# First batch's gate product in three rounded passes, with its low halves made on GpSimd

## The chip, the cores and the metric

One core of a Trainium2 chip runs the kernel. The metric is the device time of one execution in microseconds (us). The engines are TensorE (PE; its weight loads are listed apart as PEld), VectorE (DVE), ScalarE (ACT), GpSimd (POOL) and SyncE (SP, which here only issues DMAs). Each works through its own instructions in order; they are tied together by semaphores.

## The reference, cut to what matters

```python
x = L0_attn_x                                   # (16 batches, 512 tokens, 256 channels)
h = layernorm(x) * (1 + ca) + sa                # modulation of the batch
u, gate = split(h @ W_in.T)                     # the gate product is this second half
b_t = u @ W_state.T
decay = exp(-min(softplus(u @ W_dt.T + b_dt), 10) * rate)
hs = scan(decay, b_t)                           # h = d*h + (1-d)*b, over the 512 tokens
y = hs @ W_C.T
z = y * silu(gate) + h * D
x = x + ga * (z @ W_out.T)
h = layernorm(x) * (1 + cb) + sb
xr, xk = mu_r*h + (1-mu_r)*h_prev, mu_k*h + (1-mu_k)*h_prev
x = x + gb * sigmoid(xr @ W_r.T) * (square(relu(xk @ W_k.T)) @ W_v.T)
```

Everything is float32.

## The kernel before

A batch is a tile of 256 channels x 512 tokens, held as two halves (CH = 2) of 128 partitions x 512 columns. `half(outs, w, at, x, c)` (line 293 does its matmuls) multiplies input half c by the weights of each of the output halves, so a full 256 x 256 product is two calls with two matmuls each.

A product is made in one of two ways. Unsplit, both operands are float32; the profile shows each such matmul of 512 columns as two instructions. In three rounded passes, the input x is split into a rounded part x_hi (type fp32r, a copy) and x_lo = x - x_hi, the weights w likewise, and w_hi x_hi + w_lo x_hi + w_hi x_lo is summed in PSUM; each of these matmuls is one instruction. Batch 0 uses the unsplit form for its front products (dt, b), its gate product and its state output; from batch 1 on the front and gate products have three passes, and most others do from batch 2 on. The second block of the reference ("receptance" xr and "key" xk) has three passes for all batches but the last one's key.

The order on each engine is written out by hand: a prologue for batches 0 to 2, and then a loop over steps s, which works at once on batches a = s, b = s-1, c = s-2 and d = s-3. s = 3 is the first step, with d = 0, c = 1, b = 2 (WHOLE = 2).

What the change and the steps of the prediction touch:

- TensorE: in the prologue the front products of batch 0 (`w_front`), its gate product with `modulation(4, 3)` between its halves, `state_out(0)` (line 333; it waits for the scan of batch 0), `first_norm(1)` (transposes, line 300), `modulation(7, 5)`, `attention_out(0, 0)` (it waits for z of batch 0), `front_high(1)`, `front_low(1)` (which waits for both h_lo of batch 1), `attention_out(0, 1)`, `first_norm(2)`, `gate_high(1)`, `gate_low(1)`, `token_stats(0)`, `state_out(1)`, and `gate_high(2)`, which waits for `silu_ok` 2. In the loop the products of the receptance xr with the low halves xr_lo, and the state's products (lines 527, 528, 537).
- ScalarE: `modulated(0, i)` writes h of batch 0 (line 667), then `exponential(0)` (688), `decays(0)` (692, 697), a table load, `ln1_apply(1)` (658), `gate_silu(0)` (719), the rounded weights wl_hi (740), h and h_hi of batch 1 (684).
- VectorE: the rounded and low parts of the weights wf (1060 to 1065), three operations on a 128x1 rate (1067, 1069, 1071), the statistics of batch 1 (894), `clipped(0)` (983), means and variances (901), `driven(0)` (988), `scanned(0)` (996), `ln1_apply(1)` (909), statistics of batch 2, `gated(0)` (1001, and z in 1009), `ln1_apply(2)` (909), both h_lo of batch 1 (1084), the rest of the modulation, `clipped(1)`.
- GpSimd: `ln1_scale(k)` (1181 to 1188) makes the scale and shift of batch k out of VectorE's variances and is waited for by `ln1_apply(k)`; `weight_low_part(n, at)` (1203) makes wl_lo out of wl_hi; `low_part` (1173) makes xk_lo, xr_lo, k_lo; `low_state` (1227) state_lo; `second_scale(c)` (1211 to 1222) the scale of the second norm.
- The rate's sum on VectorE is `nc.vector.tensor_tensor(rate[:, 0:1], rate[:, 0:1], rate[:, 2:3], ALU.add)` (line 1069): two inputs in SBUF, one element a partition.

Of the kernel before, what the change touches and what calls it, by code (L numbers as in the profile page):

```python
# [7 lines left out]
F32 = mybir.dt.float32  # L8
F32R = mybir.dt.float32r
BF16 = mybir.dt.bfloat16  # L10
ALU = mybir.AluOpType
# [9 lines left out]
def before(eng, sem, count):  # L21

    if count > 0:
        eng.wait_ge(sem, count)

def adaln_block(nc, x_tok_d, x_ch_d, w_d, wmod_d, c_d, cols_d, ident_d, out_d):
    NB, C, T = x_ch_d.shape
    CH = C // P
    TT = T // P  # L30
    NS = P
    EXP_MAX = float(np.expm1(DT_MAX))

    with ExitStack() as ctx:
# [3 lines left out]
        def sem(name):  # L38
            return ctx.enter_context(nc.semaphore(name))
# [9 lines left out]
        wf_hi = sb("wf_hi", [P, CH, 2 * NS + C], F32R)  # L49
        wf_lo = sb("wf_lo", [P, CH, 2 * NS + C], F32R)  # L50
        wl_hi = sb("wl_hi", [P, CH, 4 * C], F32R)
        wl_lo = sb("wl_lo", [P, CH, 4 * C], F32R)
        h_hi = sb("h_hi", [P, CH, T], F32R)
        h_lo = sb("h_lo", [P, CH, T], F32R)
# [4 lines left out]
        xr_hi = sb("xr_hi", [P, CH, T], F32R)  # L59
# [140 lines left out]
        row_spread_ok, row_rstd_ok, rows_ok, offset_ok, root_ok = sem("row_spread_ok"), sem("row_rstd_ok"), sem("rows_ok"), sem("offset_ok"), sem("root_ok")  # L200
        scaled1_ok = sem("scaled1_ok")
        minus1_ok = sem("minus1_ok")
        spread1_ok, slo_ok, rstd1_ok, shift1_ok, rstd2_ok, first_ok = sem("spread1_ok"), sem("slo_ok"), sem("rstd1_ok"), sem("shift1_ok"), sem("rstd2_ok"), sem("first_ok")
        hlo_ok, zlo_ok, xklo_ok, xrlo_ok, klo_ok = sems("hlo_ok"), sems("zlo_ok"), sems("xklo_ok"), sems("xrlo_ok"), sems("klo_ok")

# [6 lines left out]
        def live(k):  # L212
            return 0 <= k < NB
# [7 lines left out]
        def split_state(k):  # L221
            return WHOLE <= k <= LAST
# [66 lines left out]
        def _(pe):  # L289
            def half(outs, w, at, x, c, first=False, last=False):  # L290

                for d, out in enumerate(outs):
                    ins = nc.tensor.matmul(out, w[:, c, at + d * P:at + (d + 1) * P], x[:, c, :], start=first, stop=last)  # L293
                return ins
# [118 lines left out]
            half(dt_out, w_front, 0, h[:, 0], 1, last=True).then_inc(dt_ps, 1)  # L413
            half(b_out, w_front, NS, h[:, 0], 0, first=True)
            half(b_out, w_front, NS, h[:, 0], 1, last=True).then_inc(b_ps, 1)
            pe.wait_ge(s_wgate, 16)
            g_out = [ps_gate(0)[:, d, :] for d in range(CH)]
            half(g_out, w_early, GATE, h[:, 0], 0, first=True)
            pe.wait_ge(s_wmod2, 16)
            modulation(4, 3, slot[2][:, 1, :])  # L420
            half(g_out, w_early, GATE, h[:, 0], 1, last=True).then_inc(g_ps, 1)
            pe.wait_ge(s_wy, 16)
            state_out(0)
            first_norm(1)
# [27 lines left out]
            for s in STEPS:  # L452
# [68 lines left out]
                if live(b):  # L521
# [6 lines left out]
                            nc.tensor.matmul(ps_y[:, i, :], wy_lo[:, i * P:(i + 1) * P], state_hi[:], start=False, stop=False)  # L528
                    else:
                        state_out(b)  # L530
                if live(d) and d > 0:
                    pe.wait_ge(xrlo_ok[1], d + 1)
                    half(r_out, wl_hi, MIX_R, xr_lo, 1, last=True).then_inc(r_ps, 1)
                if split_state(b):
# [13 lines left out]
                if live(c) and c < LAST:  # L548
                    pe.wait_ge(xn2b_ok, c + 1)
                    to_channels(ps_n, xn2, range(TT // 2, TT)).then_inc(t3_ps, 1)  # L550
                if d == 0:
                    pe.wait_ge(xrlo_ok[1], d + 1)
                    half(r_out, wl_hi, MIX_R, xr_lo, 1, last=True).then_inc(r_ps, 1)
                if d == LAST:
                    for done in xr_ok:
                        pe.wait_ge(done, d + 1)
# [79 lines left out]
        def _(act):  # L636
# [29 lines left out]
            def modulated(k, i):  # L666
                return nc.scalar.activation(h[:, k % 2, i, :], ps_h(k)[:, i, :], ACT.Identity, bias=mod_at(SHIFT1 + i, k), scale=mod_at(SCALE1 + i, k))
# [11 lines left out]
            def rounded_h(k):  # L679
                act.wait_ge(h_ok, k + 1)  # L680
                before(act, ghi_ps, k - 1)
                if k == WHOLE + 1:
                    act.wait_ge(b_ps, k)
                nc.scalar.copy(h_hi[:], h[:, k % 2]).then_inc(hhi_ok, 1)  # L684

            def exponential(k):
                act.wait_ge(dt_ps, k + 1)
                nc.scalar.activation(ps_front[:, 0, :], ps_front[:, 0, :], ACT.Exp, bias=col(B_DT)).then_inc(e_ok, 1)
# [41 lines left out]
            modulated(0, 0).then_inc(h0_ok, 1)  # L730
            act.wait_ge(t1_ps, 1)
            modulated(0, 1).then_inc(h_ok, 1)
            exponential(0)
            decays(0)
            nc.scalar.preload_act_table_set("silu_and_others")
# [433 lines left out]
        def _(pool):  # L1169
            def low_part(lo, x, hi, there, used, done, k):  # L1170
                pool.wait_ge(there, k + 1)
                before(pool, used, k)
                nc.gpsimd.tensor_tensor(lo, x, hi.bitcast(F32), ALU.subtract).then_inc(done, 1)  # L1173

            def ln1_scale(k):

                pool.wait_ge(mv1_ok, k + 1)
                before(pool, xn1a_ok, k - 1)
                before(pool, xn1b_ok, k - 1)
                if k > 0:  # L1180
                    nc.gpsimd.tensor_scalar(spread1[:, k % 2, 0, :], mv1[:, k % 2, :, 0], -1.0, None, ALU.mult)
                nc.gpsimd.tensor_scalar(spread1[:, k % 2, 1, :], mv1[:, k % 2, :, 1], EPS, None, ALU.add).then_inc(spread1_ok, 1)
                pool.wait_ge(spread1_ok, k + 1)
                nc.gpsimd.tensor_tensor(rstd1[:, k % 2], spread1[:, k % 2, 1, :], half_neg[:], ALU.pow).then_inc(rstd1_ok, 1)
                pool.wait_ge(rstd1_ok, k + 1)
                if k == 0:
                    pool.wait_ge(minus1_ok, 1)
                nc.gpsimd.tensor_tensor(shift1[:, k % 2], spread1[:, k % 2, 0, :], rstd1[:, k % 2], ALU.mult).then_inc(shift1_ok, 1)
# [12 lines left out]
            def weight_low_part(n, at):  # L1201
                pool.wait_ge(wl_hi_ok, n)
                nc.gpsimd.tensor_tensor(wl_lo[:, :, at:at + C], w_late[:, :, at:at + C], wl_hi[:, :, at:at + C].bitcast(F32), ALU.subtract).then_inc(wl_lo_ok, 1)
# [20 lines left out]
            def low_state(k):  # L1224
                pool.wait_ge(shi_ok, k - WHOLE + 1)
                pool.wait_ge(y_ps, k)
                nc.gpsimd.tensor_tensor(state_lo[:], state[:], state_hi[:].bitcast(F32), ALU.subtract).then_inc(slo_ok, 1)
# [11 lines left out]
                last.then_inc(offset_ok, 1)  # L1239

            ln1_scale(0)
            ln1_scale(1)
            pool.wait_ge(mod1_ok, 1)
            nc.gpsimd.tensor_scalar(scale_neg[:], mod[:, SCALE1:SCALE1 + CH, :], -float(np.sqrt(C)), None, ALU.mult)
            nc.gpsimd.tensor_scalar(scale_root[:], mod[:, SCALE1:SCALE1 + CH, :], float(np.sqrt(C)), None, ALU.mult).then_inc(root_ok, 1)
            weight_low_part(1, MIX_K)
            ln1_scale(2)
            weight_low_part(2, MIX_R)
            ln1_rows(WHOLE + 1)
            low_h(2, 0)  # L1250
# [9 lines left out]
            for s in STEPS:  # L1260
                a, b, c, d = s, s - 1, s - 2, s - 3
                if live(d) and d < LAST:
                    low_part(xk_lo[:, 0], xk[:, 0], xk_hi[:, 0], xkhi_ok[0], k_ps, xklo_ok[0], d)
                    low_part(xk_lo[:, 1], xk[:, 1], xk_hi[:, 1], xkhi_ok[1], k_ps, xklo_ok[1], d)
                if c == 1:
                    second_scale(c)
                if live(d):
                    low_part(xr_lo[:, 0], xr[:, 0], xr_hi[:, 0], xrhi_ok[0], r_ps, xrlo_ok[0], d)
                if b == WHOLE:
                    low_state(b)  # L1270
                if live(a + 1) and a > WHOLE + 1:
                    ln1_rows(a + 1)
                if c == LAST:
                    low_part(xr_lo[:, 1], xr[:, 1], xr_hi[:, 1], xrhi_ok[1], r_ps, xrlo_ok[1], d)
                if live(c) and c > 1:
                    second_scale(c)
                if live(d) and c != LAST:
                    low_part(xr_lo[:, 1], xr[:, 1], xr_hi[:, 1], xrhi_ok[1], r_ps, xrlo_ok[1], d)
                if split_state(b) and b > WHOLE:
                    low_state(b)  # L1280
                if live(d) and d < LAST:
                    for i in range(CH):
                        low_part(k_lo[:, i], k_act[:, i], k_hi[:, i], kact_ok, v_ps, klo_ok[i], d)
                if d == LAST:
                    pool.wait_ge(rv_ok, d + 1)
                    pool.wait_ge(s_out[d % 2], 16 * (d // 2))
                    nc.gpsimd.tensor_tensor(x2[:, d % 2, 0], rv, x1[:, d % 3, 0, :], ALU.add).then_inc(x2_ok[0], 1)
                if live(a) and a > WHOLE:
                    low_h(a, 0)
                if split(b):  # L1290
                    for i in range(CH):
                        pool.wait_ge(zhi_ok[i], b - WHOLE + 1)
                        pool.wait_ge(o_ps, b)
                        nc.gpsimd.tensor_tensor(z_lo[:, i], z[:, i], z_hi[:, i].bitcast(F32), ALU.subtract).then_inc(zlo_ok[i], 1)  # L1294
                if live(a) and a > WHOLE:
                    low_h(a, 1)
# [37 lines left out]
```

## Time and profile before

| | us |
|---|---|
| median of 3 runs | 343.72 |
| lowest, highest | 343.62, 874.88 |
| the profiled execution | 343.59 |
| its span | 341.8 |

```profile
PE 335.0 (98%) x1574; PEld 265.4 (78%) x1574; DVE 303.6 (89%) x465; ACT 292.4 (86%) x393; POOL 275.5 (81%) x274
PE   8999998999999999999999999999999999999995
PEclk9999999999999999999999999999999999999999
```

The first line is each engine's busy time, its share of the span and its instructions. The others cut the span into 40 equal slices (8.5 us each): a digit is the busy share in tenths, and PEclk is the granted clock of TensorE in tenths of full speed. A timeline row is: start, duration, engine, line, operation, output<-inputs, shapes, count, and in brackets how long the engine had idled before it and what ended that. Rows with a count are merged, and their duration is from the first start to the last end. Rows of one engine can overlap a little, since an instruction starts while the one before drains. Times are counted from the start of the span.

### The profile page before, as it was taken

The numbers are of one execution on the slowest core, as the hardware profiler recorded it, in microseconds if no ns is written. First come the engines' busy times: TensorE is split into PE (matmuls) and PEld (weight loads), VectorE is DVE, ScalarE is ACT, GpSimd is POOL, SyncE is SP. The second block draws the span as 40 slices with busy tenths as digits, with TensorE's granted clock in tenths as the row PEclk, the third lists the DMA queues.
The fourth block names the chain that finished last, engine by engine and source line by source line (L and its number), as shares of the span: only waits on it lengthen the run. The fifth ranks groups of instructions, "written<-read, shape, count | busy, mean of one in ns | idle before, by whom it ended". The sixth has DMA issues, their size and how long they took to land.

```text
span 341.8 us, 5185 instructions
## 1 busy us (share of the span) xinstructions
PE 335.0 (98%) x1574; PEld 265.4 (78%) x1574; DVE 303.6 (89%) x465; ACT 292.4 (86%) x393; POOL 275.5 (81%) x274
## 2 busy tenths in 40 slices
PE   8999998999999999999999999999999999999995
PEld 4567676788888888888888888888888888887764
DVE  3789888999999999999999999999999989887846
ACT  4486778989999999999999998999999999888484
POOL 2151879989898998989899898989899896966752
PEclk9999999999999999999999999999999999999999
DMA  7960523060513406051421505151320501010013
GB/s 276 416 226 13 172 83 104 1 221 27 186 61 112 136 18 221 11 186 63 161 85 64 186 0 186 63 186 61 102 83 14 174 3 61 1 63 0 2 60 126
DMA packets 18556, 36.00 MB, mean 105 GB/s; under 512 B 4960, under 2 KB 5728, under 8 KB 18400
## 3 DMA queue, kind: packets, MB, share of 16 engines
q1 hardware_dynamic: 17808, 35.19, 29.7%
q10 hardware_dynamic: 720, 0.48, 0.5%
q8 instruction: 13, 0.21, 0.3%
q14 instruction: 15, 0.12, 0.1%
HBM read 27.22 MB, written 8.44 MB: 104 GB/s over the span
## 4 chain that ended last, share of the span: by engine, by line
PE 89%; DVE 5%; issue 3%; ACT 2%; POOL 0%; DVEq 0%; ACTq 0%; POOLq 0%
PE slot L293 71%; PE slot L386 4%; PE slot L300 4%; PE slot L537 2%; PE slot L528 2%; PE slot L527 2%; PE slot L307 1%; PE slot L314 1%; PE slot L333 1%; DVE xk L979 1%; DVE xr L979 1%; DVE xn L945 1%; PE slot L394 1%; DVE h L940 0%; ACT prev L663 0%
## 5 line engine op out<-in xcount | busy, mean ns | idle before, releaser
L1173 POOL TENSOR_TENSOR k_lo<-k_act,k_hi 128x512 fp32r<-128x512 f32 x30 | 50.2, 1694 | 4.5 <-ACT k_act L872 4.5
L663 ACT ACTIVATE prev<-slot,mod,mix_prev 128x512 f32<-128x512 f32 x64 | 46.4, 785 | 1.3 <-PE slot L300 0.7
L293 PE MATMUL slot<-h_hi,wf_hi 128*128 128x512 f32 x120 | 43.0, 399 | 0.1
L1173 POOL TENSOR_TENSOR xr_lo<-xr,xr_hi 128x512 fp32r<-128x512 f32 x32 | 42.7, 1337 | 0.2 <-ACT xr_hi L709 0.2
L293 PE MATMUL slot<-h_hi,wf_lo 128*128 128x512 f32 x120 | 41.9, 390 | 0.0
L1173 POOL TENSOR_TENSOR xk_lo<-xk,xk_hi 128x512 fp32r<-128x512 f32 x30 | 38.6, 1315 | 3.7 <-ACT xk_hi L703 3.7
L1232 POOL TENSOR_TENSOR h_lo<-h,h_hi 128x512 fp32r<-128x512 f32 x28 | 36.5, 1305 | 1.3 <-ACT h_hi L684 1.3
L1294 POOL TENSOR_TENSOR z_lo<-z,z_hi 128x512 fp32r<-128x512 f32 x26 | 33.3, 1303 | 2.7 <-ACT z_hi L858 2.7
L293 PE MATMUL slot<-h_lo,wf_hi 128*128 128x512 f32 x120 | 34.2, 389 | 0.0
L979 DVE SCALAR_TENSOR_TENSOR xk<-slot,mix_new,prev 128x512 f32<-128x512 f32 x32 | 23.8, 746 | 8.2 <-issue 7.9
L945 DVE TENSOR_SCALAR xn<-slot,stats,rstd 128x256 f32<-128x256 f32 x62 | 29.2, 532 | 0.0
L725 ACT ACTIVATE k_act<-slot 128x1024 f32<-128x1024 f32 x15 | 15.5, 1031 | 14.1 <-PE slot L293 14.1
L293 PEld LDWEIGHTS slot<-h_hi,wf_hi 128*128 128x128 f32 x120 | 22.4, 188 | 6.1 <-issue 1.4
L293 PEld LDWEIGHTS slot<-h_hi,wf_lo 128*128 128x128 f32 x120 | 22.5, 188 | 5.3 <-issue 0.5
L1001 DVE TENSOR_TENSOR slot<-silu,slot 128x1024 f32<-128x1024 f32 x16 | 19.7, 1229 | 7.7 <-PE slot L537 6.9
L293 PEld LDWEIGHTS slot<-h_lo,wf_hi 128*128 128x128 f32 x120 | 22.5, 188 | 4.8
L979 DVE SCALAR_TENSOR_TENSOR xr<-slot,mix_new,prev 128x512 f32<-128x512 f32 x32 | 23.5, 741 | 2.6 <-ACT prev L663 2.6
L975 DVE SCALAR_TENSOR_TENSOR x<-slot,mod,x_ch 128x512 f32<-128x512 f32 x32 | 22.5, 744 | 1.3 <-PE slot L293 1.3
L1015 DVE BATCH_NORM_STATS2 stats<-slot 128x6 f32<-128x512 f32 x32 | 20.7, 690 | 2.8 <-PE slot L386 2.8
L1009 DVE SCALAR_TENSOR_TENSOR z<-h,cols,slot 128x512 f32<-128x512 f32 x32 | 22.5, 745 | 0.6
L652 ACT ACTIVATE r_gate<-slot 128x1024 f32<-128x1024 f32 x15 | 15.5, 1030 | 8.5 <-PE slot L293 8.5
L968 DVE SCALAR_TENSOR_TENSOR wmod<-slot,mod,x 128x512 f32<-128x512 f32 x30 | 21.1, 743 | 0.0
(164 smaller groups left out, 977.6 us busy)
## 6 DMA issues: line engine op xcount, KB each, us to landing
x_ch<-x_ch_in SPq DMA_DIRECT2D x16, 512.0 KB, 4.3
x_tok<-x_tok_in SPq DMA_DIRECT2D x15, 512.0 KB, 5.4
x_out<-wmod SPq DMA_DIRECT2D x15, 512.0 KB, 3.2
spread_rows<-rows_spread SPq DMA_DIRECT2D x13, 512.0 KB, 3.8
wmod<-wmod_in SPq DMA_DIRECT2D x1, 1024.0 KB, 8.5
w_in<-weights_in SPq DMA_DIRECT2D x1, 1024.0 KB, 11.2
w_in<-weights_in SPq DMA_DIRECT2D x1, 512.0 KB, 4.5
wmod<-wmod_in SPq DMA_DIRECT2D x1, 512.0 KB, 5.8
```

The lines of the kernel that those rows point to most:

```text
L293: ins = nc.tensor.matmul(out, w[:, c, at + d * P:at + (d + 1) * P], x[:, c, :], start=first, stop=last)
L663: return nc.scalar.activation(prev[:, mix, i, 1:T + 1], ps_n[:, i, :], ACT.Identity, bias=mod_at(SHIFT2 + i, k), scale=mix_prev[:, mix, i, ...
L945: last = nc.vector.tensor_scalar(xn2[:, t, :], ps_x1(k)[:, t, :], mean2(k)[:, t:t + 1], rstd2[:, k % 2, t:t + 1], ALU.subtract, ALU.mult)
L968: nc.vector.scalar_tensor_tensor(x2[:, k % 2, i], ps_v(k)[:, i], mod_at(GATE2 + i, k), x1[:, k % 3, i, :], ALU.mult, ALU.add).then_inc(x2_ ...
L975: nc.vector.scalar_tensor_tensor(x1[:, k % 3, i, :], ps_o(k)[:, i, :], mod_at(GATE1 + i, k), x_ch[:, k % 3, i, :], ALU.mult, ALU.add).then ...
L979: nc.vector.scalar_tensor_tensor(x[:, i, :], ps_n[:, i, :], mix_now[:, mix, i, k:k + 1], prev[:, mix, i, 0:T], ALU.mult, ALU.add).then_inc ...
L1001: nc.vector.tensor_tensor(ps_y[:], silu[:], ps_y[:], ALU.mult).then_inc(yg_ok, 1)
L1009: nc.vector.scalar_tensor_tensor(z[:, i, :], h[:, k % 2, i, :], col(D0 + i), ps_y[:, i, :], ALU.mult, ALU.add).then_inc(z_ok[i], 1)
L1015: last = nc.vector.bn_stats(stats2[:, k % 2, q], ps_x1(k)[:, 2 * q:2 * q + 2, :].rearrange("p t c -> p c t"))
L1173: nc.gpsimd.tensor_tensor(lo, x, hi.bitcast(F32), ALU.subtract).then_inc(done, 1)
L1232: nc.gpsimd.tensor_tensor(h_lo[:, i], h[:, k % 2, i], h_hi[:, i].bitcast(F32), ALU.subtract).then_inc(hlo_ok[i], 1)
L1294: nc.gpsimd.tensor_tensor(z_lo[:, i], z[:, i], z_hi[:, i].bitcast(F32), ALU.subtract).then_inc(zlo_ok[i], 1)
```

## The change

Five edits, in the order of time:

- ScalarE copies h of batch 0 to h_hi ahead of `exponential(0)`. `rounded_h(1)`, which writes h_hi next, gets a wait for the gate product of batch 0 (`g_ps`).
- GpSimd makes both halves of h_lo of batch 0 between `ln1_scale(0)` and `ln1_scale(1)`.
- TensorE's gate product of batch 0 is made of 8 passes over h_hi, the modulation, and 4 passes over h_lo, in place of 4 unsplit matmuls (8 instructions). It waits for wf_lo, h_hi and each h_lo; the wait for the weights' DMA is no longer there, since VectorE's split of them has it.
- GpSimd's `ln1_scale(2)` is moved ahead of `weight_low_part(1)`.
- In the loop GpSimd makes the first half of xr_lo ahead of `second_scale(1)` in the step with c = 1, and `low_state(2)` comes behind the second half of xr_lo; on TensorE the second xr_lo product of batch 0 moves from behind the transposes to ahead of the state_lo products, where the other batches have it.

```diff
             g_out = [ps_gate(0)[:, d, :] for d in range(CH)]
-            half(g_out, w_early, GATE, h[:, 0], 0, first=True)
+            pe.wait_ge(wsplit_lo, 2)
+            pe.wait_ge(first_h_hi, 1)
+            for i in range(CH):
+                half(g_out, wf_hi, 2 * NS, h_hi, i, first=(i == 0))
+                half(g_out, wf_lo, 2 * NS, h_hi, i)
             pe.wait_ge(s_wmod2, 16)
             modulation(4, 3, slot[2][:, 1, :])
-            half(g_out, w_early, GATE, h[:, 0], 1, last=True).then_inc(g_ps, 1)
+            for i in range(CH):
+                pe.wait_ge(first_h_lo, i + 1)
+                last = half(g_out, wf_hi, 2 * NS, h_lo, i, last=(i == CH - 1))
+            last.then_inc(g_ps, 1)
...
-                if live(d) and d > 0:
+                if live(d):
                     pe.wait_ge(xrlo_ok[1], d + 1)
                     half(r_out, wl_hi, MIX_R, xr_lo, 1, last=True).then_inc(r_ps, 1)
...
-                if d == 0:
-                    pe.wait_ge(xrlo_ok[1], d + 1)
-                    half(r_out, wl_hi, MIX_R, xr_lo, 1, last=True).then_inc(r_ps, 1)
...
             def rounded_h(k):
                 act.wait_ge(h_ok, k + 1)
                 before(act, ghi_ps, k - 1)
+                if k == 1:
+                    act.wait_ge(g_ps, 1)
...
             modulated(0, 1).then_inc(h_ok, 1)
+            act.wait_ge(h_ok, 1)
+            nc.scalar.copy(h_hi[:], h[:, 0]).then_inc(first_h_hi, 1)
             exponential(0)
...
             ln1_scale(0)
+            pool.wait_ge(first_h_hi, 1)
+            for i in range(CH):
+                nc.gpsimd.tensor_tensor(h_lo[:, i], h[:, 0, i], h_hi[:, i].bitcast(F32), ALU.subtract).then_inc(first_h_lo, 1)
             ln1_scale(1)
...
+            ln1_scale(2)
             weight_low_part(1, MIX_K)
-            ln1_scale(2)
             weight_low_part(2, MIX_R)
...
+                if live(d):
+                    low_part(xr_lo[:, 0], xr[:, 0], xr_hi[:, 0], xrhi_ok[0], r_ps, xrlo_ok[0], d)
                 if c == 1:
                     second_scale(c)
-                if live(d):
-                    low_part(xr_lo[:, 0], xr[:, 0], xr_hi[:, 0], xrhi_ok[0], r_ps, xrlo_ok[0], d)
-                if b == WHOLE:
-                    low_state(b)
...
-                if split_state(b) and b > WHOLE:
+                if split_state(b):
                     low_state(b)
```

## Rows read from the trace of the kernel before

**Rows 1.** Busy time by stretch: us, then each engine's busy time (instructions), clock, DMA.
```profile
80.00:100.00 20.00, 20.00 (x98) 16.59 (x97) 19.09 (x27) 18.54 (x26) 18.50 (x18) 1.00 0.31 106
```

**Rows 2.** Timeline of TensorE, 14 to 30 us.
```profile
14.49 1.88 PE L293 MATMUL slot<-h,w_in 128*128 128x512 f32 x4
16.21 1.41 PE L307 MATMUL slot<-c_silu,wmod 128*128 128x16 f32 x12
17.46 1.96 PE L293 MATMUL slot<-h,w_in 128*128 128x512 f32 x4
19.26 1.88 PE L333 MATMUL slot<-state,w_in 128*128 128x512 f32 x4
...
27.63 1.07 PE L293 MATMUL slot<-h_lo,wf_hi 128*128 128x512 f32 x4
28.54 1.88 PE L293 MATMUL slot<-z,w_in 128*128 128x512 f32 x4
```

**Rows 3.** Timeline of ScalarE, 10 to 25 us.
```profile
10.06 1.45 ACT L667 ACTIVATE h<-slot,mod 128x512 f32<-128x512 f32 x2 [1.59 <-PE slot L405]
12.97 0.66 ACT L688 ACTIVATE slot<-slot,cols 128x512 f32<-128x512 f32 x1 [1.47 <-PE slot L293]
15.05 0.63 ACT L692 ACTIVATE dt<-dt 128x512 f32<-128x512 f32 x1 [1.42 <-DVE dt L983]
...
23.54 1.05 ACT L684 CAST h_hi<-h 128x1024 fp32r<-128x1024 f32 x1
```

**Rows 4.** Timeline of VectorE, 12 to 28 us.
```profile
12.77 0.16 DVE L1069 TENSOR_TENSOR rate<-rate 128x1 f32<-128x1 f32 x1
...
17.20 1.22 DVE L996 TENSOR_TENSOR_SCAN state<-decay,slot 128x512 f32<-128x512 f32 x1
...
20.47 0.38 DVE L901 BATCH_NORM_AGGREGATE mv<-stats 128x2 f32<-128x6 f32 x4
21.18 1.23 DVE L1001 TENSOR_TENSOR slot<-silu,slot 128x1024 f32<-128x1024 f32 x1 [0.34 <-PE slot L333]
22.45 1.41 DVE L1009 SCALAR_TENSOR_TENSOR z<-h,cols,slot 128x512 f32<-128x512 f32 x2
...
25.97 1.28 DVE L1084 TENSOR_TENSOR h_lo<-h,h_hi 128x512 fp32r<-128x512 f32 x2
```

**Rows 5.** Timelines of GpSimd and VectorE, 22 to 57 us; line 909: ns min/median/max.
```profile
22.44 0.23 POOL L1181 TENSOR_SCALAR spread<-mv 128x4 f32<-128x4 f32 x1
...
24.30 1.27 POOL L1203 TENSOR_TENSOR wl_lo<-w_in,wl_hi 128x512 fp32r<-128x512 f32 x1
24.39 1.34 DVE L909 TENSOR_SCALAR xn<-x_tok,rstd,shift 128x256 f32<-128x256 f32 x1 [0.54 <-POOL shift L1188]
L909 DVE TENSOR_SCALAR xn<-x_tok,rstd,shift x4: 389/406/1337, 18.3 to 25.6; 128x256 f32<-128x256 f32 x4
...
53.32 1.29 POOL L1227 TENSOR_TENSOR state_lo<-state,state_hi 128x512 fp32r<-128x512 f32 x1
54.15 1.54 DVE L940 TENSOR_TENSOR h<-xn,offset 128x1024 f32<-128x1024 f32 x1
54.56 2.27 POOL L1173 TENSOR_TENSOR xr_lo<-xr,xr_hi 128x512 fp32r<-128x512 f32 x1
```

**Rows 6.** Timelines of ScalarE and TensorE, 33 to 38 us.
```profile
33.23 1.05 ACT L684 CAST h_hi<-h 128x1024 fp32r<-128x1024 f32 x1 [0.32 <-PE slot L293]
...
35.59 1.02 ACT L719 ACTIVATE silu<-slot 128x1024 f32<-128x1024 f32 x1
36.76 0.70 PE L293 MATMUL slot<-h_hi,wf_hi 128*128 128x512 f32 x2
```

**Rows 7.** Timeline of TensorE, 53 to 65 us: its waits.
```profile
53.41 0.72 PE L293 MATMUL slot<-xr_lo,wl_hi 128*128 128x512 f32 x2 [0.50 <-POOL xr_lo L1173]
...
56.88 0.73 PE L293 MATMUL slot<-xr_lo,wl_hi 128*128 128x512 f32 x2 [0.49 <-POOL xr_lo L1173]
...
64.59 0.70 PE L293 MATMUL slot<-xk_hi,wl_hi 128*128 128x512 f32 x2 [0.21 <-DVE xk L979]
```

More of the change, by code:

```diff
@@ L202, in adaln_block @@
         minus1_ok = sem("minus1_ok")
+        first_h_hi, first_h_lo = sem("first_h_hi"), sem("first_h_lo")
         spread1_ok, slo_ok, rstd1_ok, shift1_ok, rstd2_ok, first_ok = sem("spread1_ok"), sem("slo_ok"), sem("rstd1_ok"), sem("shift1_ok"), sem("rstd2_ok"), sem("first_ok")
@@ L415, in _ @@
             half(b_out, w_front, NS, h[:, 0], 1, last=True).then_inc(b_ps, 1)
-            pe.wait_ge(s_wgate, 16)
             g_out = [ps_gate(0)[:, d, :] for d in range(CH)]
-            half(g_out, w_early, GATE, h[:, 0], 0, first=True)
+            pe.wait_ge(wsplit_lo, 2)
[3 more added lines that the diff above has]
+                half(g_out, wf_lo, 2 * NS, h_hi, i)
             pe.wait_ge(s_wmod2, 16)
             modulation(4, 3, slot[2][:, 1, :])
-            half(g_out, w_early, GATE, h[:, 0], 1, last=True).then_inc(g_ps, 1)
+            for i in range(CH):
+                pe.wait_ge(first_h_lo, i + 1)
+                last = half(g_out, wf_hi, 2 * NS, h_lo, i, last=(i == CH - 1))
+            last.then_inc(g_ps, 1)
             pe.wait_ge(s_wy, 16)
```

## The prediction

> **What bounds the kernel now.** I read the busy time by stretches first [rows 1]: between 80 and 100 us TensorE is busy for the whole of its 20.00 us, and the page shows the stretches up to 300 us alike, so from there a change is worth only the TensorE time that it takes away, and this change touches none of it. Everything that is edited lies ahead of 60 us. So I read the timelines of the first 65 us, engine by engine. TensorE [rows 2] goes through the first batch's gate product, the modulation, the state output and batch 1 without a pause; its few waits come at 36.76 us, where ScalarE hands over [rows 6], and at 53.41, 56.88 and 64.59 us [rows 7]. The question is what shift reaches 64.59 us; behind it the shift goes unchanged to the end.
>
> **The gate product itself.** Unsplit, one half of it (c = 0) is four instructions from 14.49 to 16.21 us, 1.72 us [rows 2]; the other half is as long, and the modulation between them takes 17.46 - 16.21 = 1.25 us. Together that fills 14.49 to 19.42 (17.46 + 1.96; the start 19.26 of the next row overlaps its last pass). After the change there are 12 rounded passes. Four such passes run from 27.63 to 28.54 us [rows 2], 0.23 us each, so 12 x 0.23 = 2.73 us; with the 1.25 us and some 0.15 us for the changes of kind of product it is 4.13 us. TensorE would then be free at 18.6 instead of 19.4 us, a gain of about 0.75 us if nothing is late.
>
> **The new operations ahead of it.** ScalarE makes h_hi of batch 0. The two modulated() end at 10.06 + 1.45 = 11.51; the copy takes 1.05 us [rows 3] and ends at 12.59, and ScalarE's next work starts at 12.97 after 1.47 us of idle time. So it is hidden, with 0.4 us to spare. The weights' low halves are made by VectorE ahead of its row at 12.77 [rows 4], and so before TensorE wants them at 14.49: free. The added wait of rounded_h(1) for the gate product asks at 23.54 for something done by 19: free. GpSimd, idle then, starts on h_lo at about 12.67 and needs 1.27 us for each half (the price of the 128x512 subtraction in [rows 5]): 13.95 and 15.3 us. TensorE wants them at 17.6: in time.
>
> **What GpSimd's subtraction does to VectorE.** This is the step that I think decides. [Rows 5] show how these two engines meet. At 24.39 VectorE starts a normalisation that otherwise takes 0.41 us, GpSimd having begun a subtraction at 24.30 that ends at 25.57: it takes 1.34 us and ends at 25.73, right behind GpSimd's. At 54.15 VectorE's addition of two SBUF tensors (h) starts while GpSimd's state_lo runs until 54.60, and ends 1.09 us after that, at 55.69; GpSimd's next subtraction then takes 2.27 instead of 1.29 us. So each stands still until the other's instruction is over, and the one that waited goes next. The Trainium skill, page "SBUF — State Buffer", section "Who interferes with whom", says the same: a VectorE instruction with two SBUF inputs, or in a 2-port mode, and a GpSimd instruction that reads SBUF exclude each other for the whole instruction. By this rule one-input ones such as the statistics go on undisturbed.
>
> At 12.77 us VectorE has a tiny instruction: the 128x1 sum of line 1069 with both inputs in SBUF, 0.16 us long [rows 4]. GpSimd's first new subtraction begins 0.1 us before it and holds it until 13.95. It ends at about 14.0 instead of 12.93: 1.07 us late. Behind it on VectorE stand the rate's last step, the statistics of batch 1 and clipped(0), and ScalarE's logarithm at 15.05 had idled for exactly that clip [rows 3]; then decay, driven(0) and the scan. The whole chain is serial, so the scan ends at 18.42 + 1.07 = 19.49, and state_out(0) starts at about 19.56. TensorE, free at 18.6, waits 0.9 us, and is then 0.14 us later than before (19.42). The gain of 0.75 is gone.
>
> The next link: VectorE worked without a pause from the scan to 20.85, the means and variances of batch 2 [rows 4], so these end at 21.92. gated(0) follows at 21.95 instead of 21.18, and z ends at 23.86 + 0.77 = 24.63. GpSimd's ln1_scale(2) (22.44 to 24.30 before, 1.9 us [rows 5]) waits for the same variances: 22.0 to 23.9. The change puts weight_low_part(1) behind it: 23.9 to 25.15. VectorE's normalisation of batch 2, ready at 24.6, is held until then; its first tile ends at 25.3, GpSimd's second weight part, which waits by then, takes 25.3 to 26.6, and the second tile ends at 26.75. The two h_lo of batch 1, 1.28 us [rows 4], end at 28.05 instead of 27.25: VectorE is 0.8 us late. TensorE, only 0.14 us late so far, wanted them for front_low(1) at 27.77 and starts at 28.1 instead of 27.63: 0.5 us late.
>
> From there the two meet at the copy of h_hi(2), 33.23 us, before which ScalarE had idled 0.32 us for TensorE [rows 6]. By ScalarE's side (VectorE's clip ahead of it 0.83 us late) it is ready at 33.23 - 0.32 + 0.83 = 33.74, by TensorE's at 33.73. Copy, table load and silu(1) are serial, TensorE takes up gate_high(2) behind them [rows 6], and so all of it is 0.5 us late at 36.76. The work between 36.76 and 48 us hangs together and carries that shift.
>
> **The edits around 50 us.** TensorE idles 0.50 us for the first half of xr_lo and 0.49 for the second [rows 7]. With the first half ahead of second_scale(1) on GpSimd and the second ahead of low_state, both are there in time (the statistics for second_scale come only after the first one is done, so it pays nothing). GpSimd's slots stay as they were: the second half takes the slot of the first, state_lo keeps its own, and VectorE's h at 54.15 is held just as before. TensorE then is up to 1.0 us ahead. But at 64.59 it waits for VectorE's xk of batch 1 [rows 7], whose chain is h of batch 3 (55.69), its copy, a table load, tanh, prev and the mixing, all in order on ScalarE and VectorE. None waited for r_ps: ScalarE's tanh was held by its own table load. So the 1.0 us turns up as waits for z_hi, z_lo and xk, and the edits are worth 0; were that cover gone, 1.0 us.
>
> **Sum.** Against the profiled execution (343.59 us, its span 341.8; the median of the runs is 343.72): gate product -0.75, wait for the late scan +0.9, wait for h_lo of batch 1 +0.35, edits around 50 us 0: +0.5, so 344.1 us. Bounds of this case: if VectorE's second tile and h_lo pass ahead of GpSimd's second weight part, only +0.14 is left, 343.7; nothing in the rows shows two queued ones of VectorE against one of GpSimd, so I take the alternation and keep both ends.
>
> **Rivals.**
> (a) The small sum is not held. It would have to be dispatched ahead of GpSimd (0.1 us decides), or a one-element instruction would have to slip through; no row has one beside a running GpSimd instruction. Then the scan ends at 18.42, state_out(0) starts at 18.6, gated(0) at 20.9, z ends at 23.55. The weights' low parts still hold the normalisation (22.85 to 24.1, and 24.25 to 25.5), so h_lo(1) ends at 26.9, 0.35 us early, which is when TensorE, 0.7 us early, asks for it. Result -0.65: 342.95. Faster than before.
> (b) The 128x1 scaling of line 1071, one place behind, is held too, by GpSimd's second half, until 15.3. Then the scan ends at 20.75, h_lo(1) at about 29.3 and TensorE is 1.75 us late: 345.3. It has one input only, but so has the normalisation of [rows 5], which was held; that one has 256 elements a partition, this one has one. 
> (c) The two stalls of xr_lo are won after all, because the chain to xk moves with them: -1.0 on top, 343.1. Against it: that chain starts at VectorE's h, ahead of r_ps.
>
> **Chances.** The likeliest case 0.56; (a) 0.22; (b) 0.08; (c) 0.07, some of it together with (a), near 342; the rest, 0.07, is that other waits take up the shift, so that it stays near 343.6. Left out of the range are (b) and the end of (c) near 342: 342.8 to 344.7. The likeliest case's own range is 343.7 to 344.6. A measurement here tells about 2% from no change, 6.9 us, and all cases lie within it: same 0.96, faster 0.02, slower 0.02.
>
> **What would show it.** The gate product as 12 passes of 0.23 us; the row of line 1069 at 12.77 lasting 1.2 instead of 0.16 us; the scan ending near 19.5; TensorE waiting about 0.9 us ahead of line 333 for it; the normalisation tiles of batch 2 held near 25 us; no wait for xr_lo near 53 and 57 us, but waits for z_hi or xk between 60 and 65; first xk product of batch 1 at about 65.1 us. If line 1069 keeps its 0.16 us and line 333 starts at 18.6, case (a) holds and I am wrong by over 1 us.

## The result and the profile after

| | us |
|---|---|
| kernel before, median of 6 | 343.88 |
| changed kernel, median of 6 | 344.69 (344.32 to 345.01) |
| ratio | 1.0022, 95% interval 1.0012 to 1.0033 |
| the profiled execution of the changed kernel | 344.68, its span 342.9 |

By the 2% mark nothing changed; by the interval the kernel is 0.4 to 1.1 us slower. 344.1 had been forecast, in a range of 342.8 to 344.7, and the two medians lie 0.81 us apart where 0.5 had been expected. So the median of 344.69 is only just inside the range, and outside the 343.7 to 344.6 of the likeliest case. One of the six executions of the kernel before took 874.88 us; without it the median there is 343.72. Two lines of the page:

```profile
span 342.9 us, 5198 instructions
...
PE 334.2 (97%) x1578; PEld 265.7 (78%) x1578; DVE 304.9 (89%) x465; ACT 293.2 (86%) x394; POOL 277.3 (81%) x276
```

TensorE is busy for 0.8 us less than before (335.0) and the span is 1.1 us longer. The waits of TensorE say where that went (waiting engine and line, who ended the wait, us in total, times, longest):

```profile
PE slot L315 <- POOL zeros L1213: 1.3, 1, 1.3
PE slot L294 <- ACT z_hi L866: 1.2, 1, 1.2
PE slot L334 <- DVE state L1004: 0.8, 1, 0.8
PE slot L308 <- DMA wmod<-wmod_in: 0.4, 1, 0.4
```

The waits for xr_lo are gone and one for z_hi has come; one for VectorE's scan ahead of the state output (line 334, 333 before) is new. The wait for a DMA, and a second one of 0.4 us for w_in, are not the change's: the first loads of this execution landed later, and a second profile of the same kernel (a_repeat, below) has neither wait. The first front product starts at 11.57 us here and at 10.98 us in the execution of before. These 0.59 us have nothing to do with the edits and are taken off below wherever the two are compared. The first row is of the kernel before, the second of the changed one:

```profile
10.98 3.67 PE L293 MATMUL slot<-h,w_front 128*128 128x512 f32 x8 [0.16 <-ACT h L667]
11.57 3.67 PE L294 MATMUL slot<-h,w_front 128*128 128x512 f32 x8 [0.16 <-ACT h L671]
```

VectorE, GpSimd and ScalarE around the critical place (timelines; start, duration):

```profile
12.13 1.04 ACT L740 CAST h_hi<-h 128x1024 fp32r<-128x1024 f32 x1
13.57 0.66 ACT L694 ACTIVATE slot<-slot,cols 128x512 f32<-128x512 f32 x1 [0.39 <-PE slot L294]
13.25 1.27 POOL L1252 TENSOR_TENSOR h_lo<-h,h_hi 128x512 fp32r<-128x512 f32 x1 [5.75 <-ACT h_hi L740]
14.47 1.28 POOL L1252 TENSOR_TENSOR h_lo<-h,h_hi 128x512 fp32r<-128x512 f32 x1
13.18 0.15 DVE L1075 TENSOR_SCALAR rate<-cols 128x1 f32<-128x1 f32 x1
13.36 1.17 DVE L1077 TENSOR_TENSOR rate<-rate 128x1 f32<-128x1 f32 x1
14.57 0.15 DVE L1079 TENSOR_SCALAR rate<-rate 128x1 f32<-128x1 f32 x1
...
18.80 1.22 DVE L1004 TENSOR_TENSOR_SCAN state<-decay,slot 128x512 f32<-128x512 f32 x1
...
24.39 2.55 POOL L1211 TENSOR_TENSOR wl_lo<-w_in,wl_hi 128x512 fp32r<-128x512 f32 x2
24.93 2.17 DVE L917 TENSOR_SCALAR xn<-x_tok,rstd,shift 128x256 f32<-128x256 f32 x2
27.02 1.28 DVE L1092 TENSOR_TENSOR h_lo<-h,h_hi 128x512 fp32r<-128x512 f32 x2
```

The one thing to see is line 1077: the sum of 128x1 elements that took 0.16 us [rows 4] takes 1.17 us. GpSimd's first subtraction began at 13.25, VectorE's sum at 13.36, 0.11 us later, and the sum ends at 14.53, right behind the subtraction (13.25 + 1.27 = 14.52). The scaling of line 1079 then runs in its usual 0.15 us while the second subtraction (14.47 to 15.75) is going on. The scan starts at 18.80 instead of 17.20, which is 0.59 + 1.01 us.

TensorE's timeline in the same stretch and where the loop's edits act:

```profile
14.68 1.03 PE L294 MATMUL slot<-h_hi,wf_hi 128*128 128x512 f32 x2
...
16.91 1.40 PE L308 MATMUL slot<-c_silu,wmod 128*128 128x16 f32 x12
18.17 1.19 PE L294 MATMUL slot<-h_lo,wf_hi 128*128 128x512 f32 x4
20.17 1.95 PE L334 MATMUL slot<-state,w_in 128*128 128x512 f32 x4 [0.82 <-DVE state L1004]
21.96 1.04 PE L301 MATMUL slot<-ident,xn 128*128 128x128 f32 x8
...
28.64 1.09 PE L294 MATMUL slot<-h_lo,wf_hi 128*128 128x512 f32 x4
...
62.15 0.70 PE L294 MATMUL slot<-z_hi,wl_hi 128*128 128x512 f32 x2 [1.19 <-ACT z_hi L866]
...
65.65 0.70 PE L294 MATMUL slot<-xk_hi,wl_hi 128*128 128x512 f32 x2 [0.23 <-DVE xk L987]
```

The gate product is over at 18.17 + 1.19 = 19.36, that is 18.77 without the late loads, against 19.42 before: 0.65 us gained. TensorE then idles 0.82 us for the scan. Its state output ends at 20.17 + 1.95 = 22.12, 21.53 without the late loads. Before, it ended at 19.26 + 1.88 = 21.14 [rows 2]. So it is 0.39 us late, and that stays: 0.42 us at front_low(1) (28.64 against 27.63), 0.47 us at the first xk product of batch 1 (65.65 against 64.59 [rows 7]). From there both kernels are bound by TensorE: between 66 and 300 us it is busy for all of the 234.0 us in both.

### The profile page after: what moved, and what is told of

Its sections match the earlier page's. It is cut to its first block, busy times and chain, and to the rows that moved or that the text cites. A ratio compares the mean times of both kernels' runs of the same rounds, so it can differ in the third digit from the quotient of the medians.

```text
span 342.9 us, 5198 instructions
## 1 busy us (share of the span) xinstructions
PE 334.2 (97%) x1578; PEld 265.7 (78%) x1578; DVE 304.9 (89%) x465; ACT 293.2 (86%) x394; POOL 277.3 (81%) x276
## 4 chain that ended last, share of the span: by engine, by line
PE 85%; DVE 7%; issue 3%; DMA 2%; ACT 2%; SPq 0%; DVEq 0%; ACTq 0%
PE slot L294 69%; PE slot L387 4%; PE slot L301 4%; DMA wmod<-wmod_in 2%; PE slot L544 2%; PE slot L535 2%; PE slot L534 2%; PE slot L308 1%; PE slot L334 1%; DVE xk L987 1%; DVE xr L987 1%; DVE xn L953 1%; DVE h L948 0%; ACT prev L667 0%; DVE slot L996 0%
## 5 line engine op out<-in xcount | busy, mean ns | idle before, releaser
L294 PE MATMUL slot<-h_hi,wf_hi 128*128 128x512 f32 x124 | 44.6, 401 | 0.1
L294 PE MATMUL slot<-h_hi,wf_lo 128*128 128x512 f32 x124 | 43.2, 390 | 0.0
L1181 POOL TENSOR_TENSOR xr_lo<-xr,xr_hi 128x512 fp32r<-128x512 f32 x32 | 41.5, 1301 | 0.3 <-ACT xr_hi L715 0.3
L294 PE MATMUL slot<-h_lo,wf_hi 128*128 128x512 f32 x124 | 35.5, 391 | 0.0
L294 PEld LDWEIGHTS slot<-h_hi,wf_hi 128*128 128x128 f32 x124 | 23.1, 188 | 6.7 <-issue 1.9
L294 PEld LDWEIGHTS slot<-h_hi,wf_lo 128*128 128x128 f32 x124 | 23.3, 188 | 5.4 <-issue 0.5
L294 PEld LDWEIGHTS slot<-h_lo,wf_hi 128*128 128x128 f32 x124 | 23.2, 188 | 4.9
```

## The experiments

Beside the medians the table has a second measure, which the landing of the loads moves little: the time from TensorE's first front product of batch 0 to its first xk product of batch 1, in the profiled execution. It rests on one trace of each run; the two traces of the changed kernel agree in it to 0.01 us (65.65 - 11.57 = 54.08 and 54.08). For the kernel before it is 64.59 - 10.98 = 53.61 us. In the profiled executions of e1 and e3 TensorE's clock was at its lower level for a while (last section), so they have no entry. The first four kernels ran on one chip, the next four on another, each against the kernel before there (medians 343.96 and 343.57).

| kernel | median us | to before, us | ratio, 95% interval | front product to xk, to before |
|---|---|---|---|---|
| a_repeat | 344.31 | +0.35 | 1.0017 (1.0003 to 1.0030) | 64.97 - 10.89 = 54.08, +0.47 |
| e1_hold_freed | 343.52 | -0.44 | 0.9989 (0.9978 to 1.0001) | |
| e2_long_hold | 347.09 | +3.13 | 1.0082 (1.0057 to 1.0106) | 66.25 - 11.04 = 55.21, +1.60 |
| e3_loop_undone | 344.50 | +0.54 | 1.0012 (1.0003 to 1.0021) | |
| e4_hold_only | 344.21 | +0.64 | 1.0014 (1.0005 to 1.0022) | 64.93 - 10.89 = 54.04, +0.43 |
| e5_loop_only | 343.57 | 0.00 | 0.9998 (0.9989 to 1.0007) | 64.50 - 10.87 = 53.63, +0.02 |
| e7_table_early | 342.11 | -1.46 | 0.9958 (0.9944 to 0.9971) | 63.18 - 10.97 = 52.21, -1.40 |
| e8_table_no_loop | 342.97 | -0.60 | 0.9969 (0.9949 to 0.9988) | 63.58 - 10.93 = 52.65, -0.96 |

**a_repeat: the changed kernel again.**

> The changed kernel again, as the reference point for the three beside it. Theory H (GpSimd's first new subtraction holds VectorE's 128x1 sum): 0.4 to 0.9 us over the kernel before, that sum lasts about 1.2 us, and TensorE waits 0.8 us for the scan ahead of the state output. Theory N (the extra time is only a later landing of the first loads in that one execution): no difference to the kernel before within 0.2 us, on average.

Slower than before here too, by 0.35 us where 0.4 to 0.9 had been expected, and its first loads landed as in the profiled execution of before, so theory N, that only the landing differed, falls. The hold is the same: line 1077 takes 1.17 us in it, and the wait for the scan 0.81 us. The second measure gives +0.47 us, the same number as the first profile of the changed kernel.

**e1_hold_freed: the same work, the hold taken away.**

```diff
             ln1_scale(0)
             pool.wait_ge(first_h_hi, 1)
+            pool.wait_ge(rate_ok, 1)
             for i in range(CH):
```

> The changed kernel, with one wait more: GpSimd starts on the low halves only when VectorE's three rate operations are done, some 0.5 us later. Nothing else moves. Theory H: the 128x1 sum is back at 0.16 us, the scan ends 1.0 us earlier, TensorE runs into the state output without a wait, and the time falls 1.0 to 1.2 us below the changed kernel, to 0.5 to 0.7 us below the kernel before. Theory N: the same as the changed kernel, or slower by the 0.5 us by which GpSimd starts later.

GpSimd starts later by a wait, and the kernel becomes faster: 0.79 us below a_repeat by the medians, less than the 1.0 to 1.2 us expected. Against the kernel before it is -0.44 us, with an interval that just reaches 1, so by the medians alone faster than before is likely and not shown. VectorE's and GpSimd's timelines:

```profile
13.89 0.16 DVE L1077 TENSOR_TENSOR rate<-rate 128x1 f32<-128x1 f32 x1
14.38 2.50 POOL L1253 TENSOR_TENSOR h_lo<-h,h_hi 128x512 fp32r<-128x512 f32 x2 [6.87 <-DVE rate L1079]
```

The sum is back at 0.16 us, and TensorE has no wait for the scan any more. In this execution the low clock had delayed TensorE ahead of it, but e7 and e8, with the same wait on GpSimd and at full clock, have none either. From the first gate pass on (16.50 us, where the clock is full again) the trace can be compared: 66.39 - 16.50 = 49.89 us to the xk product, against 65.65 - 14.68 = 50.97 us in the changed kernel (and the same in a_repeat). That is 1.08 us less, inside the expected 1.0 to 1.2. That the change's loss comes from the meeting of these two instructions, and not from the work that GpSimd or ScalarE has more, is shown by this.

**e2_long_hold: the hold doubled.**

```diff
-            for i in range(CH):
-                nc.gpsimd.tensor_tensor(h_lo[:, i], h[:, 0, i], h_hi[:, i].bitcast(F32), ALU.subtract).then_inc(first_h_lo, 1)
+            nc.gpsimd.tensor_tensor(h_lo[:], h[:, 0], h_hi[:].bitcast(F32), ALU.subtract).then_inc(first_h_lo, 2)
```

> The changed kernel, with the two subtractions of 128x512 made one of 128x1024, so that the hold lasts twice as long; TensorE gets both halves at the time when it got the second. Theory H: the 128x1 sum lasts about 2.3 us, the scan ends 1.1 us later again, TensorE waits 1.9 us for it, and the time is 1.0 to 1.2 us over the changed kernel. Theory N, and any theory in which GpSimd's work and not its hold on VectorE counts: no difference.

```profile
12.78 2.36 POOL L1251 TENSOR_TENSOR h_lo<-h,h_hi 128x1024 fp32r<-128x1024 f32 x1 [5.08 <-ACT h_hi L740]
12.83 2.32 DVE L1077 TENSOR_TENSOR rate<-rate 128x1 f32<-128x1 f32 x1
20.80 1.96 PE L334 MATMUL slot<-state,w_in 128*128 128x512 f32 x4 [1.96 <-DVE state L1004]
```

One subtraction of the same size in total (2.36 us) holds a sum of one element a partition for 2.32 us, so the hold lasts as long as GpSimd's instruction does, and TensorE's wait grows to 1.96 us. By the second measure the kernel lies 1.60 - 0.47 = 1.13 us over the changed one, inside the expected 1.0 to 1.2 us. The median is 2.78 us over it. Four of the six executions have a lower mean clock, told in the last section; the two at 0.999 and 1.000 took 345.35 us on average, 1.04 us over the median of a_repeat.

**e3_loop_undone: the loop's edits taken out of the changed kernel.** The diff is the last five hunks of the change, reversed.

> The changed kernel with the edits of the loop undone (xr_lo, low_state and the product order of batch 0 as before). My theory, that the two waits of 0.5 us come back but only replace the wait for z_hi near 61 us, since the product of xk of batch 1 waits for VectorE: within 0.2 us of the changed kernel. The rival, that the two waits are won: 1.0 us over the changed kernel.

```profile
PE slot L294 <- POOL xr_lo L1184: 1.0, 2, 0.5
```

The two waits are back, 1.0 us together, and the median is 0.19 us over a_repeat, not 1.0. From the end of the state output, where this trace's clock is back at full, to xk it takes 67.39 - 23.90 = 43.49 us (23.90 = 20.25 + 3.65, last section); with the loop's edits it is 65.65 - 22.12 = 43.53.

**e5_loop_only: the loop's edits alone, on the kernel before.**

> The kernel before, with the edits of the loop alone. Theory: the two waits for xr_lo (0.50 and 0.49 us) are gone, a wait for z_hi of 1.2 us near 61 us takes their place, xk of batch 1 starts at the same time, and the time is within 0.1 us of the kernel before. Rival: 1.0 us faster.

```profile
PE slot L293 <- ACT z_hi L855: 1.1, 1, 1.1
...
61.00 0.70 PE L293 MATMUL slot<-z_hi,wl_hi 128*128 128x512 f32 x2 [1.15 <-ACT z_hi L855]
64.50 0.69 PE L293 MATMUL slot<-xk_hi,wl_hi 128*128 128x512 f32 x2 [0.21 <-DVE xk L976]
```

The same median, to the hundredth, as the kernel before. The 1.0 us of waiting has moved from 53 and 57 us to 61 us, and xk starts when it did (53.63 against 53.61 us behind the front product).

**e4_hold_only: the hold alone, on the kernel before.** ScalarE's copy and GpSimd's subtractions are made, no product uses them, and the gate product stays unsplit. `rounded_h(1)` waits for the subtractions, and `ln1_scale(2)` stays where it was.

```diff
                 before(act, ghi_ps, k - 1)
+                if k == 1:
+                    act.wait_ge(first_h_lo, 2)
...
             modulated(0, 1).then_inc(h_ok, 1)
+            act.wait_ge(h_ok, 1)
+            nc.scalar.copy(h_hi[:], h[:, 0]).then_inc(first_h_hi, 1)
...
             ln1_scale(0)
+            pool.wait_ge(first_h_hi, 1)
+            for i in range(CH):
+                nc.gpsimd.tensor_tensor(h_lo[:, i], h[:, 0, i], h_hi[:, i].bitcast(F32), ALU.subtract).then_inc(first_h_lo, 1)
```

> The kernel before, with the hold alone: ScalarE's copy of h of batch 0 and GpSimd's two subtractions are made as in the change, but nothing uses them, and the gate product stays unsplit. Theory H: VectorE's 128x1 sum lasts 1.2 us and the scan ends 1.0 us late, 0.07 us behind the moment when TensorE is free; with TensorE's restart behind a wait (0.2 us in the changed kernel's row) 0.1 to 0.3 us over the kernel before. The gate product's own gain would then be the rest of the comparison. If ScalarE's copy or GpSimd's work cost something by themselves, it is more than 0.5 us.

```profile
12.69 1.18 DVE L1074 TENSOR_TENSOR rate<-rate 128x1 f32<-128x1 f32 x1
17.37 1.96 PE L294 MATMUL slot<-h,w_in 128*128 128x512 f32 x4
19.50 1.96 PE L334 MATMUL slot<-state,w_in 128*128 128x512 f32 x4 [0.16 <-DVE state L1001]
```

More than I expected: +0.43 us by the second measure, the same as the whole change within 0.04 us. TensorE, with its longer unsplit product, waits only 0.16 us, but the state output ends just as late as in the changed kernel, because the scan sets it in both. So in the change the cheaper gate product brings nothing at all: it is spent wholly on waiting for the scan. The expectation fell short since it took the wait as 0.07 us. The median (+0.64 us) lies further above it; that part is not explained. No run takes back the move of `ln1_scale(2)` alone, but e4 does without it and comes out the same.

**e7_table_early: the hold freed, and the chain behind the loop's edits shortened.** GpSimd has the wait of e1, and ScalarE loads its table earlier:

```diff
                 if d == 0:
+                    nc.scalar.preload_act_table_set("silu_and_others")
                     rounded_h(a)
-                    nc.scalar.preload_act_table_set("silu_and_others")
```

> The changed kernel with the hold freed (GpSimd waits for the rate, as in e1) and one thing more: in the first step of the loop ScalarE loads its table ahead of the copy of h of batch 3, in the 0.75 us that it idles for VectorE there, and not behind it. Theory: the chain copy, table load, tanh, prev, mixing, xk is what TensorE waits for behind the loop's edits; it gets 0.7 us shorter, the wait for z_hi falls from 1.2 to 0.5 us, and the time is 0.6 to 0.8 us below e1, 1.0 to 1.3 us below the kernel before. Rival (the waits near 61 us have another source): the same as e1.

```profile
54.42 1.28 ACT L840 ACT_TABLE_LOAD   x1
55.72 1.05 ACT L690 CAST h_hi<-h 128x1024 fp32r<-128x1024 f32 x1
56.67 1.02 ACT L656 ACTIVATE r_gate<-slot 128x1024 f32<-128x1024 f32 x1
...
59.68 0.70 PE L294 MATMUL slot<-z_hi,wl_hi 128*128 128x512 f32 x2 [0.34 <-ACT z_hi L866]
63.18 0.69 PE L294 MATMUL slot<-xk_hi,wl_hi 128*128 128x512 f32 x2 [0.20 <-DVE xk L987]
```

The table load fills ScalarE's idle time ahead of the copy, and the wait for z_hi falls from 1.19 to 0.34 us. At 342.11 us it is 1.46 us below the kernel before, more than the 1.0 to 1.3 expected, and beats both kernels. Against e1, from the first gate pass on, the trace gives 63.18 - 14.07 = 49.11 us for 49.89, 0.78 us less, as expected. That the chain through ScalarE's table load and tanh, and not r_ps, held xk is shown by it.

**e8_table_no_loop: e7 without the loop's edits.**

> The kernel of e7 with the loop's edits undone. Theory: with the chain shortened, TensorE's own work decides again, and the two waits for xr_lo count as far as the 1.2 us of z_hi's wait had hidden them: it gains less from the early table load than e7 does, and is 0.2 to 0.5 us slower than e7. If the loop's edits are worth nothing even then, it equals e7.

By the second measure it starts xk 52.65 - 52.21 = 0.44 us later than e7, as expected; by the medians it is 0.86 us slower, with wide intervals that overlap. It has both waits for xr_lo and none for z_hi. So the loop's edits are worth nothing in the kernel before and about 0.4 us once the chain behind them is short.

## Why the prediction was right, point by point

- **The hold (right, and the step that decided).** 1.01 us more on the 128x1 sum; 1.07 had been said, since I let it end 0.05 us behind GpSimd's instruction, and the two end together (14.53 and 14.52).
- **The gate product (nearly right).** -0.65 us for -0.75. The four h_lo passes behind the modulation last 1.19 us to their end, the change of kind included, not 0.92 + 0.15.
- **The wait for the late scan (right, one part missing).** 0.82 us of waiting for 0.9. But the sum lacked a term: the state output then took 1.95 us from its start to its end, where four unsplit instructions behind running work add 1.72. Behind a wait they took 0.23 us more (1.95 or 1.96 us behind waits of 0.82, 0.16 in e4 and 1.96 in e2). Most of it is an overlap that is lost: before, the state output started at 19.26, 0.16 us ahead of the end of the gate product at 19.42 [rows 2], and behind a wait there is nothing to overlap with. The prediction set a start (19.56) against that end (19.42) and so called TensorE 0.14 us late, where start against start it is 0.30. -0.65 + 0.82 + 0.23 = +0.40, which is the 0.39 us at the end of the state output.
- **The wait for h_lo of batch 1 (wrong).** +0.35 us had been put down; TensorE did not wait there. The alternation of GpSimd's weight parts with VectorE's two normalisation tiles came as described, 2.17 us for the pair, where in the kernel before, with one of GpSimd's subtractions beside it, it was 1.66 us (24.39 to 26.05). But I had placed each VectorE instruction behind the end of the one before it, while the rows overlap by some 0.1 us each, so that VectorE was 0.46 us late at the end of h_lo (27.02 + 1.28 = 28.30, less 0.59, against 27.25) and not 0.8. With TensorE itself 0.39 us late, that is no wait. The two errors, 0.23 us left out and 0.35 us too much, nearly cancel, so the total came out right partly by luck.
- **The shift from 36 us on (right).** 0.47 us at the xk product for 0.5.
- **The edits around 50 us (right).** Worth 0, by e3 and e5; the 1.0 us reappears as the wait for z_hi, as said.
- **Rival (a)**, that the small sum is not held, fell with the row of line 1077. What it described is e1: by the medians faster than before by 0.44 us, for the 0.65 us worked out, and in e7, which has the same hold freed, the state output starts 18.60 - 10.97 = 7.63 us behind the first front product, 0.65 us less than before (19.26 - 10.98 = 8.28).
- **Rival (b)**, that line 1079 is held as well, fell: 0.15 us, at 14.57, while GpSimd's second subtraction was running.
- **Rival (c)** fell by e3 and e5.

What stays open is the size at the level of the medians: +0.81 us in the first comparison (+0.97 without the execution of 874.88), +0.35 us in a_repeat, while both profiles give +0.47. Times of either kernel differ by some tenths from one execution to the next at the same mean clock. The landing of the first loads can be a part of that (0.59 us in the two profiles above); the runs do not settle which value is the mean. That the first median is inside the range, by 0.01 us, is luck too.

## What to carry to other kernels

Before work is given to an idle GpSimd, look at what VectorE dispatches in the same microsecond, however small: here a sum of one element a partition with two SBUF inputs waited for the whole of a GpSimd subtraction of 128x512 (1.17 us) or 128x1024 (2.32 us), and everything behind it on VectorE waited too. A wait that starts GpSimd half a microsecond later can be the faster choice (e1), and two shorter GpSimd instructions did less harm than a long one (e2).

Not every pair of this kind meets like that. In the trace of a_repeat another 128x1 operation of VectorE with two SBUF inputs ran in its 0.16 us in the midst of a GpSimd instruction that raises 128x4 elements to a power, also with two SBUF inputs; e4, e5, e7 and e8 show the same.

```profile
6.37 1.04 POOL L1192 TENSOR_TENSOR rstd<-spread,half_neg 128x4 f32<-128x4 f32 x1
6.86 0.16 DVE L1060 TENSOR_TENSOR rate<-rate,cols 128x1 f32<-128x1 f32 x1
```

So the hold is measured here for GpSimd's large subtractions; what sets the two cases apart, no run shows.

A wait on the bounding engine is worth removing only as far as the next one behind it is not the same length: follow the chain to the next product before counting the gain.

## What the runs showed of the hardware that I had not expected

TensorE's granted clock fell to the lower of its two levels, 1.2 GHz, in some executions behind a short wait. In the profiled execution of e3 it did so behind the 0.81 us wait for the scan, and the state output took 3.65 us instead of 1.95. Busy time by stretch in that execution (us, then PE, PEld, DVE, ACT, POOL busy, granted clock, DMA), with the timeline's row:

```profile
18.00:20.00 2.00, 1.44 (x8) 0.91 (x7) 1.81 (x2) 1.97 (x4) 1.55 (x4) 1.00 1.06 402
20.00:22.00 2.00, 1.75 (x2) 0.83 (x3) 2.00 (x7) 2.00 (x5) 0.00 (x0) 0.57 0.43 145
22.00:24.00 2.00, 2.00 (x6) 0.83 (x5) 0.49 (x6) 0.46 (x1) 1.25 (x3) 0.58 0.67 244
24.00:26.00 2.00, 2.00 (x22) 2.00 (x19) 1.97 (x3) 1.19 (x2) 1.92 (x4) 1.00 0.00 0
...
20.25 3.65 PE L334 MATMUL slot<-state,w_in 128*128 128x512 f32 x4 [0.81 <-DVE state L1007]
```

In e1 it fell earlier, behind waits for the first loads of 0.9 and 0.6 us, which ended at 8.64 and 5.70 us:

```profile
PE slot L308 <- DMA wmod<-wmod_in: 0.9, 1, 0.9
PE slot L395 <- DMA w_in<-weights_in: 0.6, 1, 0.6
...
12.00:14.00 2.00, 2.00 (x4) 0.96 (x3) 1.93 (x6) 1.67 (x2) 0.00 (x0) 0.50 1.06 442
```

Such a wait need not do it: in e7 TensorE waited 0.8 us for w_in, until 5.78 us, and the clock of every stretch up to 300 us was 1.00.

Only these two of the kept traces show such a fall ahead of 325 us; of the other executions only the mean clock is on record. It is 0.990 to 0.995 in some, and these took 0.3 to 2.8 us more than the others of their kernel: 346.39 us (0.995) in a_repeat, for example, where ten of twelve took 343.9 to 344.6 at 0.998 to 1.000. Such executions are rare where TensorE does not wait for the scan (2 of 90: one of e1 and one of the kernel before, whose clocks are on record for 53 executions) or waits 0.16 us (e4, 0 of 11). With the wait of 0.8 us they are 5 of 30: 2 of 6 of the changed kernel, 2 of 12 of a_repeat, 1 of 12 of e3. With the 2.0 us of e2 they are 4 of 6; these took 346.89 to 348.10 us, the two others 345.13 and 345.57. So a wait on the bounding engine early in the kernel cost its length, 0.23 us behind it, and, in a share of the executions that was larger for the longer wait, up to 2.8 us more, 1.70 us of it seen in a trace (3.65 against 1.95 us in e3). That the wait is what brings the clock down is likely by these counts; where it fell in the executions without a trace is not shown.
